# Row loads six tiles ahead, norm powers between gathers, and another load order at the start

## The chip, the cores and the metric

One NeuronCore of a Trainium2 chip runs the whole program. The metric is device time in microseconds (us), and lower is better. Six engines matter: PE (TensorE, matmuls; PEld is its weight load), DVE (VectorE), ACT (ScalarE), POOL (GpSimd), and SP (SyncE), which here only issues DMAs; 16 DMA engines move the data. Engines run on their own and wait for one another by semaphores. L3012 is line 3012 of the kernel.

## What is computed

A four-layer decoder on x (8 sequences of 100 tokens, 256 features) with a context of 361 rows for each sequence. Each layer has self-attention or a scan, cross-attention and a feed-forward part, and every part is followed by a residual sum and a layer norm. The change touches the loads ahead of the first part and the last part, a mixture of experts:

```
def _L3_ffn_ref(u, g_shared, W1_s, b1_s, W2_s, b2_s, g_routed, W1_r, b1_r, W2_r, b2_r, centroids):
    E_R, E_S, K = (8, 2, 2)                       # H = 1024 hidden, C = 256 features
    h_s = _experts_mlp(u, g_shared, W1_s, b1_s, W2_s, b2_s).sum(axis=-2)
    scores = jax.nn.sigmoid(u @ centroids)
    gpk, i_topk = jax.lax.top_k(scores, K)
    gk = gpk / scores.sum(axis=-1, keepdims=True)
    routed_all = _experts_mlp(u, g_routed, W1_r, b1_r, W2_r, b2_r)   # rmsnorm, W1, gelu, W2
    routed_topk = jnp.take_along_axis(routed_all, i_topk[..., None], axis=2)
    h_r = (gk[..., None] * routed_topk).sum(axis=-2)
    return u + h_s + h_r
...
x = _layernorm(x + _L3_ffn_ref(x, ...), axis=-1)
```

## The kernel before

The program is twelve stages, one after the other, with a barrier between blocks. At the start SP issues five loads: `XT` (x with features on partitions), the first stage's weights, the tables, `X` (x with tokens on partitions) and `ctxT` (the context). SP then waits for XT, the tables and X; the block ends for all engines only then. PE's first matmuls (L1322) read XT and weights.

The last mixture sends each token to two of eight experts. The normalised tokens are scattered in DRAM (`l3f_rows`) into 20 tiles of 128 rows, each tile with rows of one expert. `routed_experts` takes the tiles in turn. A tile i is two units u = 2i and 2i+1, each of 1026 KB of weights (half of the expert's hidden features). Per unit, in program order:

- SP (`sync_load`, L2941) loads unit u+4 into one of four landing buffers (two lie in the unused `ctxT`, two are `l3f_expert`) once unit u has been used. In the odd unit of a tile it then issues `load_rows(i + 2)` (L2986): two row buffers, `l3f_routed_x_rows`. In the even unit it stores the tile before (L3000). All of these go through SP's one queue.
- PE turns the next tile's rows (L3012, two transposes, in the odd unit), does the 24 matmuls of `first` (L3024 to L3026) for this unit, and the 12 of `second` (L3038 to L3040) for the unit before. Values are split into a high and a low part, and each product takes three passes.
- ACT rounds the rows to `x_high` (L3058), the second weights to their high part (L3063), makes the gelu (L3073) and `h_high` (L3077).
- DVE splits the first weights: cast to `w_high` (L3086) and difference `w_low` (L3088), then `x_low` (L3094) once per tile, `h_low` (L3111), and the copy of a finished tile (L3101).
- POOL makes `w_low` of the second weights (L3120).

`routed_tail` follows. POOL issues 16 indirect gathers (L3141; two for each of eight sequences), and then, for each sequence, the norm's power: `vareps` (L135) and `rstd` (L137), in `rstd_pool`. DVE adds the two gathered rows with their shares (L3182), takes statistics (L113, L115), and normalises two sequences later (L122). SP stores the output.

## Time and profile before

| what | us |
|---|---|
| median of 3 runs | 2620.01 (2616.91 to 2622.92) |
| the profiled execution's own time | 2616.16 |
| its span, first to last instruction | 2614.3 |
| PE busy | 2166.2 (83%) |
| DVE busy | 1535.2 (59%) |
| POOL busy | 586.0 (22%) |
| mean granted TensorE clock | 0.886 of full |

```profile
## 4 chain that ended last, share of the span: by engine, by line
PE 4%; DMA 3%; POOL 1%; DVE 1%; issue 1%; ACT 0%; SPq 0%; DVEq 0%; ACTq 0%; POOLq 0%
```

The chain is followed back from the last instruction and here covers only the last stage; its largest share by line is the load of the row tiles, 3%. Times in the rows below are us from the span's start. The loop of the routed tiles runs from 2353 to 2576 us, the tail from there to the end. "Clock" in a stretch is the share of full speed that was granted: 1.00 is 2.4 GHz, 0.50 is 1.2 GHz.

### The profile page before, as it was taken

Reading aid. Unit: us, or ns where it says so; the run is one execution under the profiler, and the core shown is the slowest. Engines: PE = TensorE matmul, PEld = TensorE weight load, DVE = VectorE, ACT = ScalarE, POOL = GpSimd, SP = SyncE. Lnnn points to the kernel's source line nnn. Section 1 sums busy time; section 2 is a strip of 40 time slices with the busy share of each in tenths; the row PEclk is TensorE's granted clock in tenths of the full one; section 3 lists DMA queues with packets and bytes.
Section 4 is the critical chain, followed back from the end, with each engine's and each line's share of the span. In section 5 each row is a group of like instructions: output and inputs, shape, how many; then the busy total and the mean of one; then the engine's idle time right before and its main releaser. Section 6 shows DMA issues by size and latency. Waiting matters only on the chain. (4 is left out here: it accounts for less than half of the span.)

```text
span 2614.3 us, 42273 instructions
## 1 busy us (share of the span) xinstructions
PE 2166.2 (83%) x14834; PEld 1685.9 (64%) x14834; DVE 1535.2 (59%) x3631; ACT 1121.6 (43%) x3143; POOL 586.0 (22%) x725
## 2 busy tenths in 40 slices
PE   5799674668999976869978868989996999798893
PEld 3566441226777754559956538879995566598883
DVE  4566648996556553556555554545554556556865
ACT  5566344452444433533311444523332366455652
POOL 0200017992000010010022420000003222213555
PEclk9899787899999986669977979979997899697987
DMA  3000012210000003314310014322210000245762
GB/s 110 9 2 2 33 67 76 64 63 33 1 1 1 1 31 115 111 62 165 116 41 0 5 31 122 92 95 92 92 43 35 5 8 4 92 155 174 228 212 87
DMA packets 58247, 174.92 MB, mean 67 GB/s; under 512 B 18327, under 2 KB 28155, under 8 KB 56008
## 3 DMA queue, kind: packets, MB, share of 16 engines
q1 hardware_dynamic: 56012, 169.23, 20.1%
q0 software_dynamic: 2048, 3.29, 0.4%
q8 instruction: 107, 1.75, 0.3%
q14 instruction: 80, 0.66, 0.1%
HBM read 154.11 MB, written 18.38 MB: 66 GB/s over the span
## 5 line engine op out<-in xcount | busy, mean ns | idle before, releaser
L2410 PE MATMUL ps<-l1a_zc,tables_sb 128*128 128x400 f32 x256 | 108.8, 558 | 95.2 <-POOL l1a_zc L2339 60.3
L2410 PEld LDWEIGHTS ps<-l1a_zc,tables_sb 128*128 128x128 f32 x256 | 47.3, 202 | 156.6 <-POOL l1a_zc L2339 88.3
L1912 ACT ACTIVATE l1x_probs<-ps,l1x_nmax 100x361 f32<-100x361 f32 x128 | 70.7, 558 | 164.5 <-DVE l1x_nmax L1987 164.5
L2350 POOL TENSOR_TENSOR l1a_dbx<-l1a_dx,l1a_rows 128x400 f32<-128x400 f32 x128 | 130.5, 1059 | 7.0 <-DMA l1a_rows<-l1a_rows_spilled 4.9
L2363 ACT ACTIVATE ps<-l1a_delta,weights 128x400 f32<-128x400 f32 x128 | 76.5, 598 | 81.1 <-DVE ps L2393 53.1
L1026 ACT ACTIVATE l3x_probs<-l3x_s_sb,l3x_nmax 100x361 f32<-100x361 f32 x128 | 75.3, 589 | 70.4 <-DVE l3x_nmax L1115 66.4
L1024 ACT ACTIVATE l0x_probs<-ps,l0x_nmax 100x361 f32<-100x361 f32 x128 | 70.7, 557 | 65.0 <-DVE l0x_nmax L1122 56.8
L3024 PE MATMUL ps<-l3f_routed_x_high,l3f_routed_w_low 128*128 128x128 f32 x320 | 95.5, 298 | 3.5 <-DVE l3f_routed_w_low L3088 1.7
L3025 PE MATMUL ps<-l3f_routed_x_high,l3f_routed_w_high 128*128 128x128 f32 x320 | 95.3, 298 | 0.0
L3026 PE MATMUL ps<-l3f_routed_x_low,l3f_routed_w_high 128*128 128x128 f32 x320 | 95.2, 298 | 0.0
L2602 PE MATMUL ps<-l2f_x_high,l2f_w_high 128*128 128x400 f32 x272 | 95.0, 349 | 0.0
L2603 PE MATMUL ps<-l2f_x_low,l2f_w_high 128*128 128x400 f32 x272 | 94.3, 347 | 0.0
L2601 PE MATMUL ps<-l2f_x_high,l2f_w_low 128*128 128x400 f32 x272 | 94.3, 347 | 0.0
L2393 DVE TENSOR_TENSOR_SCAN ps<-ps,l1a_dbx 128x400 f32<-128x400 f32 x86 | 84.6, 994 | 16.6 <-POOL l1a_dbx L2350 9.8
L1115 DVE CUSTOM_DVE_ANT_0 l3x_s_sb<-ps,l3x_mask_b 100x361 f32<-100x361 f32 x128 | 63.2, 531 | 46.6 <-PE ps L931 46.3
L3120 POOL TENSOR_TENSOR l3f_routed_w_low<-ctxT,l3f_routed_w_high 128x1024 fp32r<-128x1024 f32 x20 | 53.6, 2680 | 121.5 <-ACT l3f_routed_w_high L3063 121.5
L1399 PE MATMUL ps<-l2x_a_kept,l2x_a_taps 100*100 100x100 f32 x768 | 75.9, 258 | 2.9 <-DMA l2x_a_taps<-l2x_taps_spread 2.6
L2758 DVE SCALAR_TENSOR_TENSOR l2f_hg<-ps,l2f_biases,l2f_act_out 128x800 f32<-128x800 f32 x34 | 35.7, 1051 | 72.4 <-PE ps L2603 72.4
L1399 PEld LDWEIGHTS ps<-l2x_a_kept,l2x_a_taps 100*100 100x100 f32 x768 | 74.3, 174 | 5.5 <-DMA l2x_a_taps<-l2x_taps_spread 3.3
L1122 DVE TENSOR_REDUCE l0x_nmax<-ps 100x2 f32<-100x722 f32 x64 | 58.2, 909 | 32.3 <-PE ps L931 32.3
L1987 DVE TENSOR_REDUCE l1x_nmax<-ps 100x2 f32<-100x722 f32 x64 | 58.0, 906 | 29.2 <-PE ps L1842 29.1
L135 POOL TENSOR_SCALAR l1x_heads_all_vareps<-l1x_heads_all_meanvar 100x1 f32<-100x1 f32 x8 | 1.7, 217 | 324.5 <-DVE l1x_heads_all_meanvar L115 324.5
(714 smaller groups left out, 6754.5 us busy)
## 6 DMA issues: line engine op xcount, KB each, us to landing
ctxT<-l_ffn_units SPq DMA_DIRECT2D x20, 1026.0 KB, 5.7
l3f_expert<-l_ffn_units SPq DMA_DIRECT2D x20, 1026.0 KB, 5.5
l2x_a_taps<-l2x_taps_spread SPq DMA_DIRECT2D x8, 1912.5 KB
l2f_landing<-l_ffn_units SPq DMA_DIRECT2D x17, 771.0 KB, 6.0
l1a_rows<-l1a_rows_spilled SPq DMA_DIRECT2D x32, 400.0 KB, 3.5
l1f_gates<-l1f_gates SPq DMA_DIRECT2D x16, 800.0 KB, 4.1
l1f_positions<-l1f_staged SPq DMA_DIRECT2D x16, 621.9 KB
l1f_landing<-l_ffn_units SPq DMA_DIRECT2D x16, 512.0 KB, 3.5
```

What stands on the lines that cost most here:

```text
L1026: last = act.activation(probs[:, n % 2, r, 0:KEYS], s_sb[:, h % 3, r % 2, :], ACT.Exp, scale=-1.0, bias=nmax[:, n % 2, r:r + 1], accum_out ...
L1399: last = pe.matmul(score_bank(r)[:, n, :], taps[:, j % 2, first:first + S], kept[:, g % 3, n, c:c + S], start=(c == 0), stop=(c == 2))
L2350: pool.tensor_tensor(dbx[:, n % BUFS, :], dx[:, j, m, :], rows[:, g % RING, 0, :], ALU.mult).then_inc(s.dbx_ready, 1)
L2363: act.activation(da(n), delta_h[:, m, j, :], ACT.Exp, scale=a_log[:, m, i:i + 1]).then_inc(s.da_ready, 1)
L2393: dve.tensor_tensor_scan(z(n), da(n), dbx[:, n % BUFS, :], 0.0, ALU.mult, ALU.add).then_inc(s.scan_done, 1)
L2410: pe.matmul(y_bank(m), st.ident, zc[:, n % DONE, :], start=(i == 0), stop=(i == NS - 1)).then_inc(s.sum_done, 1)
L2601: pe.matmul(out, r(w_lo), r(x_hi), start=start, stop=False)
L2602: pe.matmul(out, r(w_hi), r(x_hi), start=False, stop=False)
L2603: return pe.matmul(out, r(w_hi), r(x_lo), start=False, stop=stop)
L3024: pe.matmul(out, r(lo), r(x_high[i % 2][:, k, :]), start=(k == 0), stop=False)
L3025: pe.matmul(out, r(hi), r(x_high[i % 2][:, k, :]), start=False, stop=False)
L3026: last = pe.matmul(out, r(hi), r(x_low[i % 2][:, k, :]), start=False, stop=(k == KT - 1))
```

## The change

There are three edits, and one that only makes room for them (the semaphore sets shrink from 52 to 50).

1. **Rows.** The row buffers become six slots of 256 columns in `XT`, which nothing reads any more at that point. SP issues the loads of tiles 0 to 5 at the beginning and then `load_rows(i + 6)` where it issued `load_rows(i + 2)`. Each slot has its own semaphore.
2. **Powers.** In the tail POOL computes the power of sequence j-3 after the two gathers of sequence j.
3. **Beginning.** SP issues the first weights ahead of XT. X has a semaphore of its own, for which only DVE waits, at the beginning of the first stage. ctxT is issued after the first block, whose end now waits for XT and the tables alone.

```diff
-SET, LAST = 52, 11
+SET, LAST = 50, 11
...
+GATHER_LAG, ROW_SLOTS = 3, 6
...
-        x_rows = [sb(f"x_rows{i}", [P, D]) for i in range(2)]
+        x_rows = st.XT[:].rearrange("p k b t -> p (k b t)")[:, 0:ROW_SLOTS * D].rearrange("p (i d) -> p i d", d=D)
...
-                    after(sp, s.x_turned, i - 1)
-                    sp.dma_start(x_rows[i % 2][:], routes.rows[i * P:(i + 1) * P, :]).then_inc(rows_loaded[i % 2], 16)
+                    after(sp, s.x_turned, i - ROW_SLOTS + 1)
+                    sp.dma_start(x_rows[:, i % ROW_SLOTS, :], routes.rows[i * P:(i + 1) * P, :]).then_inc(rows_loaded[i % ROW_SLOTS], 16)
...
-                load_rows(0)
-                load_rows(1)
+                for i in range(ROW_SLOTS):
+                    load_rows(i)
...
-                    if h == 1 and i + 2 < N:
-                        load_rows(i + 2)
+                    if h == 1 and i + ROW_SLOTS < N:
+                        load_rows(i + ROW_SLOTS)
...
-                    pe.wait_ge(rows_loaded[i % 2], 16 * (i // 2 + 1))
+                    pe.wait_ge(rows_loaded[i % ROW_SLOTS], 16 * (i // ROW_SLOTS + 1))
...
-                for j in range(B):
-                    for k in range(K):
-                        pool.indirect_dma_start(got[:, j, k, :], None, routes.results,
-                                                bass.IndirectOffsetOnAxis(routes.row[:, j, k:k + 1], 0)).then_inc(gathered[j], 16)
-                for j in range(B):
-                    rstd_pool(pool, wide, s, j)
+                for j in range(B + GATHER_LAG):
+                    if j < B:
+                        for k in range(K):
+                            pool.indirect_dma_start(got[:, j, k, :], None, routes.results,
+                                                    bass.IndirectOffsetOnAxis(routes.row[:, j, k:k + 1], 0)).then_inc(gathered[j], 16)
+                    if j >= GATHER_LAG:
+                        rstd_pool(pool, wide, s, j - GATHER_LAG)
...
+                sp.dma_start(packs[stages[0]], dram[f"pack{stages[0]}"]).then_inc(pack_loaded[stages[0]], 16)
                 sp.dma_start(st.XT[:], dram["x_features"]).then_inc(start_loaded, 16)
-                sp.dma_start(packs[stages[0]], dram[f"pack{stages[0]}"]).then_inc(pack_loaded[stages[0]], 16)
                 sp.dma_start(st.tables[:], dram["tables"]).then_inc(start_loaded, 16)
-                sp.dma_start(st.X[:], dram["x_tokens"]).then_inc(start_loaded, 16)
-                sp.dma_start(st.ctxT[:], dram["ctx_features"]).then_inc(ctx_loaded, 16)
-                sp.wait_ge(start_loaded, 48)
+                sp.dma_start(st.X[:], dram["x_tokens"]).then_inc(x_loaded, 16)
+                sp.wait_ge(start_loaded, 32)
...
+            if n == 0:
+                nc.sync.dma_start(st.ctxT[:], dram["ctx_features"]).then_inc(ctx_loaded, 16)
...
+                if n == 0 and eng is nc.vector:
+                    eng.wait_ge(x_loaded, 16)
```

How SP's queue reads at the program's start, first before the change and then with it (XT, the weights `pack`, `tables_sb`, X and ctxT are the five loads; the branch is the end of the first block):

```order
-L4143 DMA XT<-x_features 128x1600
-L4144 DMA weights<-pack 128x2048
-L4145 DMA tables_sb<-tables 128x342
-L4146 DMA X<-x_tokens 100x2048
-L4147 DMA ctxT<-ctx_features 128x5776
-L4140 UNCONDITIONAL_BRANCH
...
+L4146 DMA weights<-pack 128x2048
+L4147 DMA XT<-x_features 128x1600
+L4148 DMA tables_sb<-tables 128x342
+L4149 DMA X<-x_tokens 100x2048
+L4143 UNCONDITIONAL_BRANCH
+L4158 DMA ctxT<-ctx_features 128x5776
```

XT and the weights have changed places, and ctxT has moved behind the end of the block.

POOL in the tail before (`l3f_got` are the gathered rows):

```order
L3141 DMA l3f_got<-l3f_results,l3f_row 100x256 x16
L135 TENSOR_SCALAR l3f_tail_all_vareps<-l3f_tail_all_meanvar 100x1
L137 TENSOR_TENSOR l3f_tail_all_rstd<-l3f_tail_all_vareps,minus_half 100x1
L135 TENSOR_SCALAR l3f_tail_all_vareps<-l3f_tail_all_meanvar 100x1
L137 TENSOR_TENSOR l3f_tail_all_rstd<-l3f_tail_all_vareps,minus_half 100x1
```

and POOL in the tail now:

```order
L3143 DMA l3f_got<-l3f_results,l3f_row 100x256 x8
L135 TENSOR_SCALAR l3f_tail_all_vareps<-l3f_tail_all_meanvar 100x1
L137 TENSOR_TENSOR l3f_tail_all_rstd<-l3f_tail_all_vareps,minus_half 100x1
L3143 DMA l3f_got<-l3f_results,l3f_row 100x256 x2
L135 TENSOR_SCALAR l3f_tail_all_vareps<-l3f_tail_all_meanvar 100x1
L137 TENSOR_TENSOR l3f_tail_all_rstd<-l3f_tail_all_vareps,minus_half 100x1
```

The first power stands behind eight gathers in place of sixteen, and four powers now stand ahead of the last two gathers. In the routed loop SP's queue keeps its order, a row load behind every second unit of weights; only the first group of row loads grows from two to six, and the last six tiles need no further load.

## Rows read from the trace of the kernel before

**Rows 1.** which engine line waited for whom, 2350 to 2575 (us in total, times, longest)
```profile
PE ps L3012 <- DMA l3f_routed_x_rows<-l3f_rows: 22.9, 15, 4.9
```

**Rows 2.** stretches of the loop: length; busy us PE, PEld, DVE, ACT, POOL; clock; DMA
```profile
2398.10:2411.80 13.70, 13.70 (x67) 13.70 (x66) 6.03 (x10) 5.89 (x13) 2.27 (x2) 0.50 0.54 176
...
2432.30:2439.10 6.80, 6.80 (x35) 6.80 (x33) 4.67 (x6) 2.36 (x6) 1.21 (x1) 0.50 0.66 203
...
2439.10:2524.40 85.30, 73.80 (x626) 71.60 (x625) 69.52 (x76) 55.27 (x119) 47.20 (x18) 1.00 0.73 234
...
2524.40:2541.50 17.10, 17.10 (x81) 17.10 (x82) 7.92 (x11) 6.50 (x15) 4.24 (x2) 0.50 0.51 153
```

**Rows 3.** PE in order of time: start us, us, instruction [idle before <-releaser]
```profile
2375.75 0.44 PE L3012 MATMUL ps<-tables_sb,l3f_routed_x_rows 128*128 128x128 f32 x2 [0.48 <-DMA l3f_routed_x_rows<-l3f_rows]
...
2396.25 0.44 PE L3012 MATMUL ps<-tables_sb,l3f_routed_x_rows 128*128 128x128 f32 x2 [1.78 <-DMA l3f_routed_x_rows<-l3f_rows]
...
2431.15 0.44 PE L3012 MATMUL ps<-tables_sb,l3f_routed_x_rows 128*128 128x128 f32 x2 [1.50 <-DMA l3f_routed_x_rows<-l3f_rows]
...
2448.22 0.30 PE L3024 MATMUL ps<-l3f_routed_x_high,l3f_routed_w_low 128*128 128x128 f32 x1 [0.92 <-DVE l3f_routed_w_low L3088]
...
2452.52 0.44 PE L3012 MATMUL ps<-tables_sb,l3f_routed_x_rows 128*128 128x128 f32 x2
...
2483.59 0.44 PE L3012 MATMUL ps<-tables_sb,l3f_routed_x_rows 128*128 128x128 f32 x2 [1.82 <-DMA l3f_routed_x_rows<-l3f_rows]
...
2524.35 0.65 PE L3012 MATMUL ps<-tables_sb,l3f_routed_x_rows 128*128 128x128 f32 x2 [1.79 <-DMA l3f_routed_x_rows<-l3f_rows]
...
2560.70 0.44 PE L3012 MATMUL ps<-tables_sb,l3f_routed_x_rows 128*128 128x128 f32 x2 [1.31 <-DMA l3f_routed_x_rows<-l3f_rows]
```

**Rows 4.** DVE in order of time, one tile at full clock with no row wait
```profile
2443.79 0.69 DVE L3086 CAST l3f_routed_w_high<-ctxT 128x1024 fp32r<-128x1024 f32 x1
...
2444.51 3.09 DVE L3088 TENSOR_TENSOR l3f_routed_w_low<-ctxT,l3f_routed_w_high 128x1024 fp32r<-128x1024 f32 x1
...
2451.35 1.22 DVE L3088 TENSOR_TENSOR l3f_routed_w_low<-ctxT,l3f_routed_w_high 128x1024 fp32r<-128x1024 f32 x1
...
2453.43 0.68 DVE L3086 CAST l3f_routed_w_high<-l3f_expert 128x1024 fp32r<-128x1024 f32 x1
```

**Rows 5.** the first stretches of the program, columns as in Rows 2
```profile
0.00:5.00 5.00, 0.00 (x0) 0.00 (x0) 0.00 (x0) 0.00 (x0) 0.29 (x5) 1.00 0.63 218
...
5.00:8.00 3.00, 0.00 (x0) 0.00 (x0) 0.00 (x0) 0.00 (x0) 0.00 (x0) 1.00 1.16 432
```

**Rows 6.** all engines in order of time, the beginning
```profile
14.69 0.34 SPq L4157 DMA_DIRECT2D weights<-pack  x1
...
15.12 7.58 PE L1322 MATMUL ps<-XT,weights 128*128 128x400 f32 x16 [15.12 <-PEq L4140]
...
21.39 1.18 DVE L1575 TENSOR_SCALAR l0a_q_pad<-ps,tables_sb 128x400 f32<-128x400 f32 x2 [21.39 <-PE ps L1322]
```

**Rows 7.** DMA issues: KB each, median us from issue to landing
```profile
weights<-pack SPq DMA_DIRECT2D x1, 1024.0 KB, 6.8
...
l3f_got<-l3f_results,l3f_row POOLq DMA_INDIRECT x16, 2.9
```

**Rows 8.** all engines in order of time, the last mixture's tail
```profile
2598.70 1.01 POOL L3141 DMA_INDIRECT l3f_got<-l3f_results,l3f_row  x1 [0.30 <-issue]
...
2599.78 0.25 POOL L135 TENSOR_SCALAR l3f_tail_all_vareps<-l3f_tail_all_meanvar 100x1 f32<-100x1 f32 x1
...
2600.69 0.21 POOL L135 TENSOR_SCALAR l3f_tail_all_vareps<-l3f_tail_all_meanvar 100x1 f32<-100x1 f32 x1
...
2600.73 0.41 DVE L122 TENSOR_SCALAR X<-l3f_tail_all_resid,l3f_tail_all_meanvar,l3f_tail_all_rstd 100x256 f32<-100x256 f32 x1 [10.49 <-POOL l3f_tail_all_rstd L137]
...
2608.63 1.00 DVE L3182 SCALAR_TENSOR_TENSOR l3f_tail_all_resid<-l3f_got,l3f_share,l3f_tail_all_resid 100x256 f32<-100x256 f32 x2
...
2611.38 0.41 DVE L122 TENSOR_SCALAR X<-l3f_tail_all_resid,l3f_tail_all_meanvar,l3f_tail_all_rstd 100x256 f32<-100x256 f32 x1 [0.46 <-POOL l3f_tail_all_rstd L137]
```

More of the change, by code:

```diff
@@ L2964, in routed_experts @@
         y_rows = [sb(f"y_rows{i}", [P, D]) for i in range(2)]
-        sems = ["rows_loaded0", "rows_loaded1", "x_turned", "x_cut", "x_split", "w1_cut", "w1_split", "w2_cut", "w2_split",
+        sems = [f"rows_loaded{i}" for i in range(ROW_SLOTS)] + ["x_turned", "x_cut", "x_split", "w1_cut", "w1_split", "w2_cut", "w2_split",
                 "h_ready", "gelu_done", "h_cut", "h_split", "second_done", "y_copied"]
         with stage_sems(nc, sems) as s, nc.Block(no_gpsimd_drain=True) as block:
-            rows_loaded = [s.rows_loaded0, s.rows_loaded1]
+            rows_loaded = [s.rows_loaded0, s.rows_loaded1, s.rows_loaded2, s.rows_loaded3, s.rows_loaded4, s.rows_loaded5]
             w1 = lambda part, u, q, k, m: part[u % 2][:, q, (2 * k + m) * P:(2 * k + m + 1) * P]
@@ L3008, in turn_rows @@
                 def turn_rows(i):
-                    pe.wait_ge(rows_loaded[i % 2], 16 * (i // 2 + 1))
+                    pe.wait_ge(rows_loaded[i % ROW_SLOTS], 16 * (i // ROW_SLOTS + 1))
                     after(pe, s.x_split, i - 1)
                     for k in range(KT):
-                        last = pe.transpose(x_bank(i)[:, k, :], x_rows[i % 2][:, k * P:(k + 1) * P], st.ident)
+                        last = pe.transpose(x_bank(i)[:, k, :], x_rows[:, i % ROW_SLOTS, k * P:(k + 1) * P], st.ident)
                     last.then_inc(s.x_turned, 1)
@@ L4133, in program @@
         ctx_loaded = ctx.enter_context(nc.semaphore("ctx_loaded"))
+        x_loaded = ctx.enter_context(nc.semaphore("x_loaded"))
         half_set = ctx.enter_context(nc.semaphore("half_set"))
```

## The prediction, made before the changed kernel was run

> **What bounds the kernel now.** I read the chain of waits first. It ends in the routed loop and the tail, and its largest line is the load of the row tiles. So I asked who waited for whom in the loop: PE's turn of the rows waited 15 times for that DMA, 22.9 us in all, 4.9 of them at the loop's start [rows 1]. That leaves 18.0 us in 14 waits inside the loop. The reason stands in the code: a row load is issued right behind a 1026 KB unit of weights on the same queue, and PE wants it one and a half units later.
>
> PE in order of time shows the single waits, 0.48 to 1.82 us, and the rhythm: seven turns from 2452.52 to 2524.35 us, so 10.26 us per tile at full clock [rows 3]. But the loop is not bound by PE alone. Around 2444 to 2454 there is no row wait, and a tile still takes 2453.43 - 2443.79 = 9.64 us [rows 4]. There DVE has no idle time: the same difference (L3088) takes 1.22 us alone and 3.09 us when POOL runs its own split beside it [rows 4], so each of POOL's two splits per tile costs DVE 1.87 us. I take 9.64 us as the pace. PE then waits 0.92 us for DVE [rows 3]. That is the bound behind the rows.
>
> The third view is the granted clock by stretches. It fell three times in the loop, for 13.7, 6.8 and 17.1 us, 37.6 us in all, from 1.00 to 0.50, that is from 2.4 to 1.2 GHz [rows 2]. The last long row wait ahead of each fall was 1.78, 1.50 and 1.79 us [rows 3]. A wait of 1.82 us at 2483.59 was followed by no fall [rows 3], so a long wait makes a fall possible and not certain. Through 0.48 and 0.92 us the clock held.
>
> **The change, part 1, the rows.** With six slots a row tile is asked for some five tiles before its turn, against a landing time of a few us, so all 14 waits inside the loop go. The wait at the loop's start stays: tile 0 is still the first load. It is followed by five more of 128 KB instead of one, and SP's next issue has to wait until the first unit is used. The total number of loads is the same, and nothing new is queued ahead of a unit of weights.
>
> What is late next is DVE's split of the first weights, at 9.64 us per tile. From the turn at 2375.75 to the last one at 2560.70 there are 17 tiles in 184.95 us [rows 3]. Afterwards they take 17 x 9.64 = 163.9 us and begin 0.48 us earlier: 21.5 us less. This counts that the clock stays at full speed, since the only waits left are near 0.92 us. How much of it is the clock: the three low stretches hold 67 + 35 + 81 = 183 matmuls [rows 2] of 74 per tile (72 and two turns), so 2.5 tiles in 37.6 us where 9.64 each would be 23.8. That is 13.8 us from the clock and 7.7 us from the waits. From the last turn on no row wait is left, and that piece stays.
>
> Bounds: the pace of PE alone is the busy share of the long full-speed stretch, 73.80 of 85.30 us [rows 2], times 10.26 = 8.88 us per tile, so at best 17 x 0.76 = 12.9 us more. I don't take it: without the row wait POOL's split starts earlier against DVE's, and falls on a DVE instruction in both units, as it does in the stretch of rows 4. At worst the clock falls as before and 13.8 us are not gained.
>
> **Part 2, the powers.** Before, the first normalisation waits 10.49 us for POOL, which has all 16 gathers ahead of the first power; then DVE works without a pause from 2600.73 to the end [rows 8]. Afterwards DVE has done sequences 0 to 4 while POOL gathers, and the last gather decides. One power costs 2600.69 - 2599.78 = 0.91 us on POOL, and four of them now stand ahead of the last gather, which starts at 2598.70 + 3.64 = 2602.34 [rows 8]. It lands 2.9 us later [rows 7], some 0.15 us pass to DVE, and from the last addition's start to the end of the last normalisation it is 2611.79 - 2608.63 = 3.16 us [rows 8]. The end is at 2608.55 against 2611.79: 3.2 us less. Bounds: 4.4 if the powers fit into the 0.30 us pauses between gathers in part, 1.0 if each costs half a us more. No gather waits for a power: with a distance of three sequences the statistics are long there.
>
> In the trace every gather takes about the same 1.01 us, also those beside DVE's additions; none stood beside a normalisation. The Trainium skill, page SBUF — State Buffer, section Who interferes with whom, speaks against this edit: tensor_scalar can enter a mode that takes the port pair shared with GpSimd, and a gather issued by GpSimd then can't write its descriptors. By that rule each of the five normalisations now beside gathers could hold POOL for its 0.41 us. No run here shows it yet. The tail would then save 3.2 - 2.0 = 1.2 us.
>
> **Part 3, the beginning.** SP's wait ends at 14.69 and PE starts at 15.12 [rows 6]. XT, the weights and the tables are 0.82 + 1.05 + 0.18 = 2.04 MB. In the first 8 us the queues moved 5 x 218 + 3 x 432 = 2.39 MB [rows 5], and the weights, the second load, landed 6.8 us after their issue at 1.20, at 8.0 [rows 7]. X, behind these, held the block. The tables land between 8.0 and 9 us; with the same 0.43 us from the release to PE and some 0.4 to the release, PE starts near 9.7: 5.4 us less, bounds 4.8 and 6.2. What hides X: DVE's first instruction is at 21.39 [rows 6], so it would be at 16.0, and X is there by 14.69 even at today's pace. If X came later, DVE alone would wait for the difference. ctxT is issued behind the block and is first wanted by the second stage, some 100 us later; the order of bytes on the queue hardly changes.
>
> **The sum.** 21.5 + 3.2 + 5.4 = 30.1 us, from the profiled execution's 2616.2: 2586.1 us. That execution lies 3.9 us below the median of its three runs, which gives 2590.0 when the difference is taken over in full. A part of that spread is where the clock falls in the other stages, and the loop's falls are part of what goes, so I say 2588 us.
>
> **The rivals.**
>
> The clock keeps falling. For it: a wait of 0.92 us by DVE in each tile stays, and the clock has fallen in this kernel after 1.50. Against it: it held from 2439.10 to 2524.40 with waits up to 1.82 inside. It costs 13.8 us: 2602.
>
> POOL and DVE fall apart in time. Then one of the two splits per tile is free of the other, and the pace comes near PE's 8.88 us: 2588 - 12.9, about 2575. For it: in late tiles of the loop DVE has such free splits of 1.22 us. Against it: that is where the row wait makes room.
>
> The gathers wait for the normalisations, the mechanism told above: the tail saves 1.2 us, and the time is 2590.
>
> Slower than before. DVE's wait in every tile makes the low clock the rule in the loop: a tile at low clock takes 13.70 / 67 x 74 = 15.1 us [rows 2], 5.5 more than 9.64. To lose the 32 us of the forecast against the median it takes six tiles of 17 at low clock, seven to be slower by what can be told. With nine it is 2588 + 50 = 2638. For it speaks only that DVE's wait comes at each tile; against it that PE is busier than before between the waits.
>
> That the rows come no sooner (XT not free, or a slot waiting for its turn) I give nothing: the wait on the slot is on a turn five tiles back.
>
> **How the numbers follow.** Forecast 2588, chance 0.55, own range 2582 to 2595. Gathers held, 2590, 0.14. Clock falls as before or in part, up to 2602, 0.16. PE's pace, 2575, 0.10. Slower, 0.02. The rest, 0.03, is a change within 0.2% (5.2 us, about what can be told from none here), if several gains fail at once. So faster has 0.95. The range 2577 to 2603 leaves out the far ends of the two middle rivals.
>
> **What would show it.** Right: no row wait at the turn of rows except the first, turns of rows 9.64 us apart, DVE without idle time in the loop, the loop at clock 1.00 throughout after the low stretch at its start; PE's first matmul near 9.7; one power after gather 8 and a last addition near 2605.5 less what is gained before. Wrong: stretches at 0.50 in the middle of the loop, turns 8.9 or over 10 us apart, gathers longer than 1.01 us beside a normalisation, or DVE held at the beginning.

## The result and the profile after

| | before | after |
|---|---|---|
| median of 4 runs, same chip (us) | 2621.06 (2616.91 to 2622.92) | 2591.91 (2590.41 to 2596.03) |
| ratio | | 0.9889 [0.9863, 0.9915] |
| the profiled execution, its span (us) | 2616.16, 2614.3 | 2590.41, 2588.6 |

The kernel is 29.2 us faster; 2588 was forecast. The profiled spans differ by 25.7 us, and that difference can be split by four marks in the two traces: the first matmul, the first turn of rows, the issue of the loop's last store of results, the end.

| piece | before | after | less | forecast |
|---|---|---|---|---|
| start to the first matmul | 15.12 | 9.42 | 5.7 | 5.4 |
| first matmul to the first turn of rows | 2340.57 | 2337.97 | 2.6 | 0 |
| first turn of rows to the last store's issue | 220.67 | 205.00 | 15.7 | 21.5 |
| last store's issue to the end | 37.95 | 36.22 | 1.7 | 3.2 |

The marks that stand in none of the rows above, first before and then after the change:

```profile
2355.69 0.69 PE L3012 MATMUL ps<-tables_sb,l3f_routed_x_rows 128*128 128x128 f32 x2 [4.87 <-DMA l3f_routed_x_rows<-l3f_rows]
...
2576.36 0.32 SPq L3004 DMA_DIRECT2D l3f_results<-l3f_routed_y_rows  x1
```

```profile
2347.39 0.69 PE L3013 MATMUL ps<-tables_sb,XT 128*128 128x128 f32 x2 [5.04 <-DMA XT<-l3f_rows]
...
2552.39 0.32 SPq L3005 DMA_DIRECT2D l3f_results<-l3f_routed_y_rows  x1
```

So the beginning came as forecast, the loop and the tail gave 7.3 us less than forecast, and the stages between gave 2.6 that no part of the change had asked for.

The chain of waits of the changed kernel, from its page: shares of the span, by engine and then by line.

```profile
DVE 5%; PE 2%; issue 1%; POOL 1%; DMA 0%; ACT 0%; DVEq 0%; POOLq 0%
DVE l3f_routed_w_low L3089 2%; DVE l3f_routed_w_high L3087 1%; POOL l3f_got L3143 1%; PE ps L3025 1%; PE ps L3027 1%; PE ps L3026 1%; DVE l3f_routed_h_low L3112 0%; DVE l3f_routed_x_low L3095 0%; DVE l3f_routed_y_rows L3102 0%; PE ps L3039 0%; PE ps L3041 0%; PE ps L3040 0%; DMA l3f_got<-l3f_results,l3f_row 0%; POOL l3f_tail_all_rstd L137 0%; DMA XT<-l3f_rows 0%
```

The row tiles' load, which led this chain before, now stands last with 0%, and DVE's split of the first weights has its place: the bound behind the rows is in front. (Lines of the loop are one higher than before: L3088 is now L3089.) The waits of the changed kernel from 2320 to 2550 us (us in total, times, longest) answer to [rows 1]:

```profile
POOL l3f_routed_w_low L3121 <- ACT l3f_routed_w_high L3064: 156.7, 40, 58.7
...
PE ps L3025 <- DVE l3f_routed_w_low L3089: 14.2, 15, 1.3
...
PEld ps L3013 <- DMA XT<-l3f_rows: 5.4, 1, 5.4
```

Of 15 waits for rows one is left, at the loop's start, and 15 waits for DVE are new. In all PE waited 18.0 us for rows in the loop before, and waits 14.2 for DVE now. POOL, on the other hand, idles for most of the loop and waits for ACT.

DVE of the changed kernel in order of time, one tile (start us, us, instruction); it answers to [rows 4]:

```profile
2400.18 0.68 DVE L3087 CAST l3f_routed_w_high<-l3f_expert 128x1024 fp32r<-128x1024 f32 x1
2400.90 3.09 DVE L3089 TENSOR_TENSOR l3f_routed_w_low<-l3f_expert,l3f_routed_w_high 128x1024 fp32r<-128x1024 f32 x1
...
2405.03 2.69 DVE L3087 CAST l3f_routed_w_high<-l3f_expert 128x1024 fp32r<-128x1024 f32 x1
2407.75 1.23 DVE L3089 TENSOR_TENSOR l3f_routed_w_low<-l3f_expert,l3f_routed_w_high 128x1024 fp32r<-128x1024 f32 x1
...
2409.83 0.68 DVE L3087 CAST l3f_routed_w_high<-ctxT 128x1024 fp32r<-128x1024 f32 x1
```

and POOL in the same stretch:

```profile
2400.53 2.38 POOL L3121 TENSOR_TENSOR l3f_routed_w_low<-ctxT,l3f_routed_w_high 128x1024 fp32r<-128x1024 f32 x1 [3.01 <-ACT l3f_routed_w_high L3064]
2404.98 2.19 POOL L3121 TENSOR_TENSOR l3f_routed_w_low<-l3f_expert,l3f_routed_w_high 128x1024 fp32r<-128x1024 f32 x1 [2.07 <-ACT l3f_routed_w_high L3064]
```

A tile takes 2409.83 - 2400.18 = 9.65 us, and no DVE instruction has a wait in brackets. POOL's first split falls on the difference (3.09 instead of 1.23 us), its second on the cast (2.69 instead of 0.68).

The stretches of the changed kernel's loop by the granted clock, columns as in [rows 2]:

```profile
2344.40:2371.70 27.30, 22.86 (x107) 22.49 (x107) 15.30 (x17) 10.64 (x23) 6.78 (x3) 0.50 0.39 120
2371.70:2426.30 54.60, 49.90 (x425) 48.64 (x424) 50.71 (x52) 36.20 (x81) 29.71 (x12) 1.00 0.76 248
2426.30:2429.70 3.40, 3.40 (x18) 3.40 (x17) 2.53 (x2) 1.26 (x3) 0.75 (x1) 0.50 0.46 157
2429.70:2494.60 64.90, 59.25 (x506) 57.86 (x505) 61.40 (x61) 43.45 (x95) 35.03 (x14) 1.00 0.77 250
2494.60:2498.00 3.40, 3.40 (x18) 3.40 (x18) 2.68 (x4) 1.42 (x4) 0.00 (x0) 0.50 0.41 125
```

The three falls of 13.7, 6.8 and 17.1 us are gone. Two of 3.4 us are new, and the low stretch at the loop's start lasts 27.3 us; before it was 17.1. The waits ahead of the two short falls, from PE in order of time:

```profile
2423.90 0.30 PE L3025 MATMUL ps<-l3f_routed_x_high,l3f_routed_w_low 128*128 128x128 f32 x1 [0.84 <-DVE l3f_routed_w_low L3089]
...
2492.04 0.30 PE L3025 MATMUL ps<-l3f_routed_x_high,l3f_routed_w_low 128*128 128x128 f32 x1 [0.93 <-DVE l3f_routed_w_low L3089]
```

The beginning, all engines in order of time, against [rows 6]:

```profile
8.98 0.35 SPq L4158 DMA_DIRECT2D ctxT<-ctx_features  x1
...
9.42 6.78 PE L1322 MATMUL ps<-XT,weights 128*128 128x400 f32 x14 [9.42 <-PEq L4143]
...
15.56 0.63 DVE L1575 TENSOR_SCALAR l0a_q_pad<-ps,tables_sb 128x400 f32<-128x400 f32 x1 [15.56 <-PE ps L1322]
```

DVE is held by PE, not by X, so X is indeed hidden. Its loads (KB each, median us from issue to landing) of the first 20 us, against [rows 7]:

```profile
ctxT<-ctx_features SPq DMA_DIRECT2D x1, 2888.0 KB, 11.4
...
weights<-pack SPq DMA_DIRECT2D x1, 1024.0 KB, 4.9
XT<-x_features SPq DMA_DIRECT2D x1, 800.0 KB, 6.3
...
tables_sb<-tables SPq DMA_DIRECT2D x1, 171.0 KB, 6.8
```

The tables are issued at 1.68 and so land at 8.5; SP is released by 8.98 and PE starts 0.44 us after that.

The tail of the changed kernel, all engines in order of time, against [rows 8]:

```profile
2575.76 1.16 POOL L3143 DMA_INDIRECT l3f_got<-l3f_results,l3f_row  x1 [0.30 <-issue]
...
2576.96 0.25 POOL L135 TENSOR_SCALAR l3f_tail_all_vareps<-l3f_tail_all_meanvar 100x1 f32<-100x1 f32 x1
2577.29 0.57 POOL L137 TENSOR_TENSOR l3f_tail_all_rstd<-l3f_tail_all_vareps,minus_half 100x1 f32<-100x1 f32 x1
2577.90 0.41 DVE L122 TENSOR_SCALAR X<-l3f_tail_all_resid,l3f_tail_all_meanvar,l3f_tail_all_rstd 100x256 f32<-100x256 f32 x1 [1.18 <-POOL l3f_tail_all_rstd L137]
2578.08 1.23 POOL L3143 DMA_INDIRECT l3f_got<-l3f_results,l3f_row  x1 [0.21 <-issue]
2578.97 1.00 DVE L3184 SCALAR_TENSOR_TENSOR l3f_tail_all_resid<-l3f_got,l3f_share,l3f_tail_all_resid 100x256 f32<-100x256 f32 x2 [0.66 <-DMA l3f_got<-l3f_results,l3f_row]
2579.61 1.25 POOL L3143 DMA_INDIRECT l3f_got<-l3f_results,l3f_row  x1 [0.30 <-issue]
...
2582.89 1.01 DVE L3184 SCALAR_TENSOR_TENSOR l3f_tail_all_resid<-l3f_got,l3f_share,l3f_tail_all_resid 100x256 f32<-100x256 f32 x2 [0.65 <-DMA l3f_got<-l3f_results,l3f_row]
...
2585.66 0.41 DVE L122 TENSOR_SCALAR X<-l3f_tail_all_resid,l3f_tail_all_meanvar,l3f_tail_all_rstd 100x256 f32<-100x256 f32 x1 [0.46 <-POOL l3f_tail_all_rstd L137]
```

DVE's wait of 10.49 us is gone. The first eight gathers take 1.01 us as before; the last eight, each pair of which now stands behind a power, take 1.15 to 1.25.

### The profile page after: what moved, and what is told of

The parts are those of the page before. It is cut to its first block and busy times, and to the rows that moved or that the text cites. A ratio compares the mean times of both kernels' runs of the same rounds, so it can differ in the third digit from the quotient of the medians.

```text
span 2588.6 us, 42273 instructions
## 1 busy us (share of the span) xinstructions
PE 2152.8 (83%) x14834; PEld 1675.5 (65%) x14834; DVE 1553.4 (60%) x3631; ACT 1120.6 (43%) x3143; POOL 582.1 (22%) x725
## 5 line engine op out<-in xcount | busy, mean ns | idle before, releaser
L3025 PE MATMUL ps<-l3f_routed_x_high,l3f_routed_w_low 128*128 128x128 f32 x320 | 92.7, 290 | 15.7 <-DVE l3f_routed_w_low L3089 14.2
L3025 PEld LDWEIGHTS ps<-l3f_routed_x_high,l3f_routed_w_low 128*128 128x128 f32 x320 | 65.1, 203 | 19.7 <-DVE l3f_routed_w_low L3089 16.9
L1987 DVE TENSOR_REDUCE l1x_nmax<-ps 100x2 f32<-100x722 f32 x64 | 57.9, 905 | 29.2 <-PE ps L1842 29.1
## 6 DMA issues: line engine op xcount, KB each, us to landing
l1f_landing<-l_ffn_units SPq DMA_DIRECT2D x16, 512.0 KB, 3.5
```

Source lines behind the costliest of these rows:

```text
L3025: pe.matmul(out, r(lo), r(x_high[i % 2][:, k, :]), start=(k == 0), stop=False)
```

## The experiments

My theory: the rows gained most; the loop is now paced by DVE, whose instructions are lengthened by POOL's splits running beside them; the tail gains less than forecast because gathers are longer beside normalisations; the beginning is worth its own 5 to 6 us. The rivals: the gain of the rows is a matter of the place (XT) or of six slots and not of asking earlier; the loop's pace of 9.64 us is PE's own or the DMA's; the gathers are longer for another reason. A "turn" below is PE's turn of a row tile; the loop is counted from the first turn to the issue of the last store of results, the tail from there to the end, always in the profiled execution.

**rows_only.** The changed kernel with the tail and the beginning of before:

```
-                for j in range(B + GATHER_LAG):
+                for j in range(B):
...
+                for j in range(B):
+                    rstd_pool(pool, wide, s, j)
...
-                sp.dma_start(st.X[:], dram["x_tokens"]).then_inc(x_loaded, 16)
-                sp.wait_ge(start_loaded, 32)
+                sp.dma_start(st.X[:], dram["x_tokens"]).then_inc(start_loaded, 16)
+                sp.dma_start(st.ctxT[:], dram["ctx_features"]).then_inc(ctx_loaded, 16)
+                sp.wait_ge(start_loaded, 48)
```

> The kernel before with the row slots alone; the tail and the beginning as before. Theory (the row wait hid behind it a bound of DVE and POOL together): the loop from the first turn of rows to the last store's issue takes about 205 us (the changed kernel's 205.0) where the kernel before took 220.7; DVE has no idle time at full clock and the turns lie 9.64 us apart; the total is 15 to 22 us below the kernel before, depending on how long the clock stays low at the loop's start. Rival (most of the gain comes from the clock in other stages and from the beginning): under 10 us.

Measured: 2601.20 us (2598.43 to 2606.34), ratio 0.9929 [0.9901, 0.9956] against 2619.57. The loop takes 205.87 us, the tail 38.01, all gathers of the second half 1.01 us, and PE waits 14 times for DVE's difference, 13.8 us in all. The rows alone are 18.4 us of the whole, and the loop is the one of the changed kernel: this part of the theory held.

**tail_only.** The changed tail, with two row buffers and the old beginning:

```
-        x_rows = st.XT[:].rearrange("p k b t -> p (k b t)")[:, 0:ROW_SLOTS * D].rearrange("p (i d) -> p i d", d=D)
+        x_rows = [sb(f"x_rows{i}", [P, D]) for i in range(2)]
-                    if h == 1 and i + ROW_SLOTS < N:
+                    if h == 1 and i + 2 < N:
...
-                sp.wait_ge(start_loaded, 32)
+                sp.wait_ge(start_loaded, 48)
```

> The kernel before with the powers between the gathers alone. Theory (each gather that is issued after the first power takes 1.15 to 1.25 us and not 1.01): the tail from the last store's issue to the end of the span takes 36.2 us where the kernel before took 38.0, 1.8 us less. The total can't be told from the kernel before (under 0.2%). Rival (the longer gathers come from the earlier clock or from the loop's change): gathers of 1.01 us throughout and 3.2 us less.

Measured: 2619.76 us over ten runs, ratio 1.0008 [0.9987, 1.0030]. In time it can't be told from before; in the trace the tail is 36.08 us instead of 37.95, with the last eight gathers at 1.05 to 1.23. The rows' waits are all there (16 in the loop, 19.7 us). So the tail's piece is real, 1.9 us, and smaller than the scatter of the whole.

**start_only.** The changed beginning, with two row buffers and the old tail:

```
+        x_rows = [sb(f"x_rows{i}", [P, D]) for i in range(2)]
...
-                for j in range(B + GATHER_LAG):
+                for j in range(B):
...
+                for j in range(B):
+                    rstd_pool(pool, wide, s, j)
```

> The kernel before with the new load order alone. Theory: PE's first matmul is at 9.4 us where it was at 15.1, DVE's first instruction at 15.6, X is there by then, and the whole program ends 5.7 us earlier except for what the clock does in the stages between (plus or minus 4). Rival (the second stage or DVE waits later for ctxT or X and gives it back): the first instruction of the second stage is not 5 us earlier than at 112.5.

Measured: 2616.23 us over ten runs, ratio 0.9985 [0.9958, 1.0013]. The first matmul starts at 8.94, 6.2 us before that of before, and DVE at 15.79. But the second stage starts at 111.92, against 112.51. That is the sign I had set for the rival, and yet neither DVE nor the second stage waited for X or ctxT: the first stage took 5.6 us longer, and that by its clock, which was at 0.50 for 36.4 us of it instead of 21.8 (at half pace 7.3 us). Over the twelve profiles of this study it took 97.4 to 102.5 us with the old order of loads (four profiles) and 97.5 to 104.0 with the new one (eight), longer where the low stretches were longer. The 6 us are there at the first matmul; in the time of the whole I can show 3.3 us with an interval that holds zero.

**slots3.** Is it six slots, or enough of them? In the changed kernel:

```
-GATHER_LAG, ROW_SLOTS = 3, 6
+GATHER_LAG, ROW_SLOTS = 3, 3
...
```

> The changed kernel with three row slots in place of six. Theory (a row load lands 5 to 6 us after its issue, and three slots give it a tile more than two, at least 9.6 us): no wait at a turn of rows beyond the first, the same pace of 9.64 us, the same time as the changed kernel within its noise. Rival (the depth matters, because rows stand behind a unit of weights each time): row waits come back, some tenths of a us at each turn, and the time is 3 to 10 us above the changed kernel.

Measured: 2592.47 us (2586.78 to 2593.88), ratio 0.9892 [0.9862, 0.9921]. No row wait in the loop, turns mostly 9.64 us apart, loop 205.21. Three slots do what six do: with one slot more than before, a load is issued one tile, that is two units of weights, earlier, and it lands before its turn.

**pool_twice.** If DVE's pace is made by POOL's splits beside it, POOL working twice as long must slow a tile although nothing waits for it first. POOL writes the same difference twice.

```
+                    pool.tensor_tensor(r(w_low[u % 2][:, :, off2:offb]), ..., ALU.subtract).then_inc(s.w2_once, 1)
+                    pool.wait_ge(s.w2_once, u + 1)
                     pool.tensor_tensor(r(w_low[u % 2][:, :, off2:offb]), ..., ALU.subtract)...
...
```

> The changed kernel in which POOL does its subtraction for the second weights twice in a row (the same values written twice). POOL then works 2 x 2.2 us in a unit of 4.82 us, so by its own time it would still keep up. Theory (POOL and DVE exclude each other for the whole of each instruction): each further split costs DVE 1.87 us, so turns lie 9.64 + 3.74 = 13.4 us apart at full clock, and the loop takes about 270 us. Rival (the 3.09 us of L3089 have another cause, and POOL only has to be done in time): turns 9.6 to 10.2 us apart, the loop under 217 us.

Measured: one run, 2674.32 us. The loop takes 275.43 us. Turns come 8.7 to 8.9 and 18.2 to 18.8 us apart in alternation: from the sixth turn to the last one 14 tiles take 191.0 us, so 13.6 per tile. Its waits from 2350 to 2640 us:

```profile
PE ps L3025 <- DVE l3f_routed_w_low L3089: 49.7, 18, 4.5
...
PE ps L3039 <- POOL l3f_routed_w_low L3124: 2.8, 1, 2.8
```

PE waits three and a half times as long as in the changed kernel for DVE, and once for POOL itself. DVE in order of time:

```profile
2409.94 2.35 DVE L3087 CAST l3f_routed_w_high<-ctxT 128x1024 fp32r<-128x1024 f32 x1
2412.32 3.08 DVE L3089 TENSOR_TENSOR l3f_routed_w_low<-ctxT,l3f_routed_w_high 128x1024 fp32r<-128x1024 f32 x1
...
2415.84 2.13 DVE L3112 TENSOR_TENSOR l3f_routed_h_low<-l3f_routed_hidden,l3f_routed_h_high 128x512 fp32r<-128x512 f32 x1
2417.90 2.67 DVE L3087 CAST l3f_routed_w_high<-ctxT 128x1024 fp32r<-128x1024 f32 x1
2420.61 1.23 DVE L3089 TENSOR_TENSOR l3f_routed_w_low<-ctxT,l3f_routed_w_high 128x1024 fp32r<-128x1024 f32 x1
```

Now a cast, a difference, a small difference and the next cast in a row are all long; each is 1.5 to 2.0 us longer than alone. The low clock is a consequence too: 111 us of it in this loop. For that reason the 13.6 us, so near the 13.4 that I had worked out for full clock, are partly luck: over these 14 tiles DVE is busy for 12.3 us a tile, 2.7 more than 9.6, and for the rest it waits, mostly for ACT, which follows the slower PE.

**pool_half.** The other way: POOL splits half the second weights (from the third unit on, the low part of the other half is left out and keeps what was written for the first two).

```
+                    n = 2 if u < 2 else 1
-                    pool.tensor_tensor(r(w_low[u % 2][:, :, off2:offb]), ...
+                    pool.tensor_tensor(r(w_low[u % 2][:, 0:n, off2:offb]), ...
```

> The changed kernel in which POOL subtracts only half of the columns of the second weights from the third unit on (the low part of the other half is left stale, so part of the computation is left out). Theory (exclusion of POOL and DVE): each split holds DVE for half as long, DVE's need falls to 9.64 - 1.87 = 7.8 us per tile, and PE is the bound at 8.8 to 8.9 us; no wait of PE for L3089. Rival (DVE is bound by itself): turns stay near 9.6 us apart.

Measured: one run, 2574.22 us; loop 183.12, turns 8.68 to 8.71 us apart from the third one on, no wait of PE for L3089. Its DVE in order of time:

```profile
2400.44 2.19 DVE L3089 TENSOR_TENSOR l3f_routed_w_low<-l3f_expert,l3f_routed_w_high 128x1024 fp32r<-128x1024 f32 x1
...
2404.45 1.22 DVE L3089 TENSOR_TENSOR l3f_routed_w_low<-l3f_expert,l3f_routed_w_high 128x1024 fp32r<-128x1024 f32 x1
```

With half the work on POOL the difference is lengthened by 0.97 instead of 1.87 us. So in both directions DVE's time follows POOL's.

**act_cast.** A version that should be better: DVE's cast of the first weights (0.68 us alone, 2.69 beside POOL) goes to ACT, which in the changed kernel is busy for 105 of 160 us (2375 to 2535).

```
+                def cut_first(u):
+                    weights_here(act, u)
+                    after(act, s.h_ready, 2 * (u - 1))
+                    act.activation(r(w_high[u % 2][:, :, 0:off2]), landing[u % R][:, :, 0:off2], ACT.Copy).then_inc(s.w1_cut, 1)
...
+                    if u + 2 < U:
+                        cut_first(u + 2)
-                    dve.tensor_copy(r(w_high[u % 2][:, :, 0:off2]), landing[u % R][:, :, 0:off2]).then_inc(s.w1_cut, 1)
```

> The changed kernel with the cast of the first weights on ACT instead of DVE, ahead of ACT's cast of the second weights. Theory (the pace of 9.64 us per tile is DVE's own 5.9 us plus two splits of POOL at 1.87 us during which DVE stands still): DVE loses 2 x 0.71 us per tile and its remaining split (L3089) ends before POOL's begins, so PE bounds the loop: turns about 8.8 to 9.0 us apart, DVE with idle time, the loop 9 to 13 us shorter than 205. Rival (ACT has no room: with the two casts it needs about 8.8 us per tile by its own durations, and the order of its queue delays the gelu): turns 9.6 us apart or more, no gain or a loss of a few us.

Measured: 2573.34 us (2570.37 to 2582.06), ratio 0.9809 [0.9762, 0.9856] to before. All its runs lie below all those of the changed kernel, the median by 18.6 us. The loop takes 183.21 us, and 11 of its last 17 tiles take 8.44 to 8.46 each. Its stretches from 2359.2 on, columns as in [rows 2]:

```profile
2359.20:2376.30 17.10, 13.91 (x64) 13.54 (x65) 7.35 (x9) 10.12 (x20) 4.55 (x2) 0.50 0.39 113
2376.30:2540.00 163.70, 160.60 (x1397) 159.56 (x1396) 99.27 (x129) 144.80 (x298) 92.79 (x38) 1.00 0.77 252
```

and the chain of its page:

```profile
PE 7%; POOL 1%; issue 0%; DMA 0%; DVE 0%; ACT 0%; DVEq 0%; POOLq 0%
```

PE is busy for 98% of the long stretch, DVE for 61%, at clock 1.00 without a fall, with 252 GB/s against the 248 and 250 of the changed kernel. So neither the DMA nor PE had set 9.64 us; and with the cast gone PE itself is the bound in 11 of 17 tiles, at 8.45, under the 8.88 that I had worked out for it. The other six take 8.75 to 9.39, and the mean is 8.71. In each of these six ACT's new cast waits 0.88 to 1.60 us for a unit of weights, and behind it stand ACT's rounding of the rows, DVE's `x_low` and PE. ACT's waits for the landing buffers in `ctxT` (those for the other two sum to 4.9 us in 7 waits), and one of the six:

```profile
ACT l3f_routed_w_high L3069 <- DMA ctxT<-l_ffn_units: 8.1, 7, 1.6
```

```profile
2415.88 1.06 ACT L3069 ACTIVATE l3f_routed_w_high<-ctxT 128x1024 fp32r<-128x1024 f32 x1 [1.25 <-DMA ctxT<-l_ffn_units]
```

So here the landing of the weights is the next bound behind PE. I had expected a loop 9 to 13 us shorter; it is 21.8 us shorter than in the changed kernel, 16.8 in the 17 tiles, 1.4 behind the last turn, and 3.6 at the loop's start, where the low stretch was the short one of 17.1 us. The last piece is chance, as the next section says, and no gain of the cast.

**act_cast_two.** Does the ACT cast help the kernel before, or do the two bounds lie one behind the other? The same edit on before, with its two row buffers.

> The kernel before, with its two row buffers, its tail and its beginning, and the cast of the first weights on ACT. Theory (two bounds lie one behind the other: the row wait at 10.3 us per tile, and DVE with POOL at 9.64 us): the row load still starts after the unit's gelu and lands 5.5 us later, so turns stay 9.8 to 10.4 us apart at full clock, PE waits for the rows 1.3 to 2 us at each turn, and the loop takes 210 to 225 us as before. Rival (each of the two gives its share by itself): turns under 9.6 us apart and the loop under 208 us.

Measured: 2620.14 us over ten runs, ratio 0.9994 [0.9971, 1.0017]. The waits from 2320 to 2600 us:

```profile
PE ps L3013 <- DMA l3f_routed_x_rows<-l3f_rows: 28.2, 13, 4.9
```

DVE's waits are gone here as well, but PE waits 23.3 us for rows inside the loop where it waited 18.0 before, up to 4.37 at a time, and low clock fills 73 us of the loop. The profiled execution (2629.57 us) was one of the slower of the ten; its loop takes 230.9 us, where I had expected 210 to 225. An edit worth 18 us behind the rows is worth nothing that can be told in front of them: the wait for rows had to go first, and that is what the change did.

**norm_late.** In the tail: are the gathers longer because a normalisation stands beside them? All eight normalisations come after the additions.

```
-def all_norms_vector(dve, wide, s, add):
+def all_norms_vector(dve, wide, s, add, lag=NORM_LAG):
...
-                all_norms_vector(dve, wide, s, add_shares)
+                all_norms_vector(dve, wide, s, add_shares, 8)
```

> The changed kernel with all eight normalisations of the tail after the eight additions; POOL's order of gathers and powers stays. Theory (a gather issued while DVE normalises is held up): all gathers back at 1.01 us, the last one starts about 23.4 us after the first where it was 24.7; the tail itself gets longer at its end, by the six normalisations that now stand behind the last addition. Rival (the powers between them or DVE's additions make the gathers longer): the gathers after the first power still take 1.15 to 1.25 us.

Measured: one run, 2598.12 us; tail 38.19 us, as the normalisations all come at the end. The gathers 9 to 16 take 1.13, 1.24, 1.12, 1.01, 1.12, 1.24, 1.12, 1.01. All engines in order of time:

```profile
2578.83 0.57 POOL L137 TENSOR_TENSOR l3f_tail_all_rstd<-l3f_tail_all_vareps,minus_half 100x1 f32<-100x1 f32 x1
2579.62 1.12 POOL L3143 DMA_INDIRECT l3f_got<-l3f_results,l3f_row  x1 [0.22 <-issue]
...
2581.05 1.24 POOL L3143 DMA_INDIRECT l3f_got<-l3f_results,l3f_row  x1 [0.30 <-issue]
...
2584.86 1.01 POOL L3143 DMA_INDIRECT l3f_got<-l3f_results,l3f_row  x1 [0.30 <-issue]
```

I had expected 1.01 throughout, and that was wrong. A gather right behind a power takes 1.12 us with no normalisation anywhere; with one beside it, in the changed kernel, 1.22 or 1.23. So the power costs 0.11 and the normalisation 0.10. The normalisation begins 0.18 us ahead of the gather and ends 0.23 us into it (2577.90 + 0.41 against 2578.08), so the 0.10 us are not the price of a whole normalisation beside a gather.

The second gather of a pair takes 1.01 or 1.24 in turn, and the rows of DVE beside it tell the two apart: it is held by DVE's addition. An addition that began ahead of the gather and ends x us into it makes it take x + 0.88 or 0.89 us; this holds for all 24 such gathers of the twelve traces with x from 0.16 to 0.38. In the changed kernel, for instance, x is 0.26, 0.33, 0.27 and 0.36 (the last is 2578.97 + 1.00 against 2579.61 in the rows of the tail), and the gathers take 1.15, 1.22, 1.16 and 1.25. Where the addition ends within 0.12 us of the gather's start, or begins behind it, the gather takes 1.01; that was so for all gathers before the change. Twice, in this run, the addition had begun only 0.06 us ahead: then the gather took 1.01, and the pair of additions 1.04 instead of 1.00. This is read from the traces; no run tests it by itself. It means that the rival named in the expectation, DVE's additions, fits the second gathers.

**act_cast_tail.** act_cast with the powers later, so that only two of them and two normalisations stand ahead of the last gather:

```
-GATHER_LAG, ROW_SLOTS = 3, 6
+GATHER_LAG, ROW_SLOTS = 5, 6
...
-                all_norms_vector(dve, wide, s, add_shares)
+                all_norms_vector(dve, wide, s, add_shares, 4)
```

> The changed kernel with the cast on ACT, the powers five sequences behind the gathers instead of three, and the normalisations of the tail four sequences behind the additions instead of two. Theory (POOL bounds the tail, and two powers of 0.91 us and their effect on the next gathers go from ahead of the last gather): the last gather starts 2.0 to 2.3 us earlier against the first, the six powers behind it give 0.7 us of that back, and the tail takes 34.4 to 34.8 us where it took 36.1; the loop 183 us as with the cast on ACT alone. Rival (the powers left to the end cost what they save): 36 us or more. The total can't be told from the kernel with the cast on ACT alone.

Measured: 2574.94 us (2567.43 to 2577.56), ratio 0.9810 [0.9778, 0.9842]. The tail takes 34.81 us against 36.10 in act_cast, and only gathers 13, 15 and 16 are longer than 1.01. So 1.3 us come back in the tail. The time can't be told from act_cast's: the scatter of either kernel's runs is larger than that, and in the profiled execution the low stretch at the loop's start was a long one (27.3 us).

## Why the prediction was right, point by point

**The rows, no wait left but the first.** Right (1 of 15 left), and rows_only shows that it is worth 18.4 us by itself. That the number of slots is not what counts, slots3 shows.

**DVE beside POOL as the next bound, 9.64 us a tile.** Right to 1%: the 17 tiles that I had put at 163.9 us took 164.9. Three runs show the cause from three sides (pool_twice 13.6, pool_half 8.69, act_cast 8.71 on the mean), two of them by a single execution each, with differences far above the scatter. In the forecast each of POOL's splits cost DVE's difference 1.87 us; in fact the second one falls on the cast and costs 2.0 (2.69 against 0.68 us).

The Trainium skill, page SBUF — State Buffer, section Who interferes with whom, says that a VectorE instruction with two inputs from SBUF competes with a GpSimd instruction that reads SBUF, and that a cast can take both ports of the pair for its whole length. The trace agrees with both (3.09 against 1.23 us, and 2.69 against 0.68).

**What was too large in the 21.5 us of the loop.** The 15.7 us that came fall short by 5.8. From the turns in the two traces: the 17 tiles gave 20.0 us, where 21.0 were forecast (1.0 short); between the second and the third turn 3.0 were lost (15.81 against 12.77 us), where 0.5 were to be gained (3.5 short); and behind the last turn 1.3 were lost, where nothing was to change.

- *"Through 0.48 and 0.92 us the clock held"* was the step that failed. It fell after waits of 0.84 and 0.93 us, twice of 15 times, each time for 3.4 us, and not after the three waits of 1.27 to 1.29. In rows_only it fell three times and in norm_late four times inside the loop, for 3.4 us each, behind waits of 0.86 to 1.31. The tile in which it falls takes 11.08 or 10.92 us instead of 9.64, and the next one 8.56 or 8.68, since DVE has run ahead; the third is 9.99 or 9.97. Over three tiles that is 0.7 us for a fall, 1.4 for both, and two tiles at the start were 0.3 faster than the pace.
- *"After the low stretch at its start"*: I took the stretch over as it was, 17.1 us. It became 27.3. PE does the same work there in both kernels; of the 10.2 us more, 9.2 lie behind the first turn, which at half pace would be 4.6 us, and 3.5 of them show. In the twelve profiles of this study the clock fell near the first turn of rows in every one: where it fell 2.7 to 3.0 us ahead of that turn (after, rows_only, slots3, act_cast_tail), it came back 24.3 to 24.6 us behind it; where it fell 0.3 to 2.2 us ahead (the eight others), it came back 14.9 to 16.8 us behind. act_cast and act_cast_tail have the same code up to there and fell on different sides, and norm_late, whose code up to there is the changed kernel's, fell on the short one. So I take these 3.5 us for chance and not for a property of the change; what decides it is open, and so is why the kernels with two row buffers (four profiles) were all on the short side.
- *"From the last turn on ... that piece stays"*: it grew by 1.3 us. The last turn itself comes without the wait of 1.31 us that stood before it [rows 3], and PE waits for DVE behind it instead. The wait was moved past the mark, not removed.

**The tail, 3.2 us.** The path was right (powers between gathers, DVE working meanwhile, the last gather decides); the size was 1.7, 1.9 in tail_only. The term mis-sized is the last gather: I had put its issue 23.42 us after the first one's (19.78 and four powers of 0.91), and it came 24.66 after (2554.95 to 2579.61), since eight gathers together took 9.69 us instead of 8.08, less shorter pauses. Of these 1.6 us, 0.45 go to the powers, 0.42 to the normalisations and 0.72 to the additions, which now stand at another point of the gathers than before. The remaining 0.25 us are the landing and the last normalisation. The prediction took the 1.01 us beside the additions as a sign that they cost nothing; but in the trace before none that had begun ahead of a gather reached more than 0.12 us into it. The price by the rule of the Trainium skill (SBUF — State Buffer, Who interferes with whom), a whole normalisation of 0.41 us for each gather, gave 1.2 us saved. The traces agree with its mechanism, as a gather ends later the later the DVE instruction ahead of it ends; the price was too high for the normalisations, of which four and not five stood beside a gather, each with only its last 0.23 us (0.10 us of cost), and the additions weren't in it.

**The beginning, 5.4 us.** 5.7 at the first matmul, and X hidden as said: no wait of DVE for it. In the time of the whole it is not shown: the 3.3 us of start_only come with an interval that holds zero, as the first stage scatters by 6.6 us with its clock.

**The rivals.** PE's pace (2575) didn't come by itself, since POOL's splits do fall on DVE in both units; act_cast and pool_half are that rival, brought about, and it stands where it was put: 2573 and 2574 us, at 8.7 us a tile. "The clock keeps falling" was true in part, for 6.8 us instead of 37.6. "Gathers held" was true in its mechanism, and the 1.7 us saved lie nearer to its 1.2 than to 3.2. The slower one needed a low clock in half the tiles; pool_twice shows what that looks like: waits of 1.8 to 4.5 us, and 111 us of low clock.

**The sum.** For the profiled execution 2586.1 us were worked out, and 2590.41 came. The loop fell short by 5.8 and the tail by 1.5; the beginning gave 0.3 and the stages between 2.6 that were not in the sum. Of the last I know only that the low stretches ahead of the loop's own sum to 508.6 us instead of 512.0, which at half pace is 1.7; the rest is open. That 2591.91 came within 4 us of 2588 is in part luck: 7.3 us fell short, and 2.9 came on top of what the terms had.

## What to carry to other kernels

When the largest wait of a chain goes, look for a stretch in the old trace that was free of it: its pace is the next bound (here 9.64 us, met within 0.01), and what runs beside the bound engine in that stretch says how to go on, as moving one cast to a less busy engine gave 18.6 us more (some of it chance: 3.6 us at the loop's start in the profiled execution). Test such an edit behind the first bound, for in front of it the same edit gave a ratio of 0.9994 [0.9971, 1.0017]. And a piece of 2 to 6 us is to be read in its own stretch of the trace: in the time of the whole it is lost among stretches of low clock that come and go.

## What the runs showed of the hardware

- A cast of 128x1024 on DVE takes 0.68 us alone and 2.35 to 2.69 beside a POOL split, a difference 1.22 and 3.09; the added time is nearly POOL's own (2.19 to 2.38), so where the two engines' instructions stand beside each other their times nearly add up, though they work on different tiles.
- The clock fell from 1.00 to 0.50 for 3.4 us after waits of only 0.84 and 0.93 us in a loop where PE was busy for 147 of 160 us, and after most waits of the same length, and after three of 1.27 to 1.29, it did not. In rows_only and norm_late it fell likewise behind waits of 0.86 to 1.31. At the loop's start the low stretch over equal work of PE lasted 17.1 or 27.3 us, by when it began.
- An indirect gather right behind a power on POOL takes 1.12 us, otherwise 1.01, and 1.22 with a normalisation on DVE that ends 0.23 us into it. An addition on DVE that began earlier and ends x us into a gather makes it take x + 0.88 or 0.89 us (24 gathers, x from 0.16 to 0.38); up to 0.12 it costs nothing.
